# Three small networks' first layer: four products and a bias product become three products with the biases as rows

## The reference, cut to what matters

```python
U = (mu @ W_dec + b_dec).reshape(B, IN_DIM + 1, 30); param = einsum('bik,kj->bij', U, V)
x = x + (x @ param[:, :-1] + param[:, -1])
```

```python
def _mlp_ln(s, W1, b1, W2, b2, g, b):
    h = silu(s @ W1 + b1) @ W2 + b2
    return _ln(h, g, b)
m = x + _mlp_ln(memory_state, mem_W1, mem_b1, ...)[:, None, :]    # 256 inputs
n = x + _mlp_ln(noise_state, noi_W1, noi_b1, ...)[:, None, :]     # 64 inputs
r = x + _mlp_ln(resource_state, res_W1, res_b1, ...)[:, None, :]  # 32 inputs
```

## Time and profile before

| what | value |
| --- | --- |
| median of 3 runs | 608.56 us (607.65 to 608.61) |
| profiled execution | 608.91 us |
| its span, first to last instruction | 607.1 us |
| PE busy | 576.7 us, 95% |
| DVE, POOL, ACT busy | 431.5, 389.4, 200.1 us |
| granted TensorE clock, mean | 0.997 of full speed |

### The profile page before, as it was taken

One profiled execution on the slowest core, in us unless ns is written; L12 is line 12 of the kernel. 1 busy time (PEld: TensorE's weight loads), 2 busy tenths in 40 slices (PEclk: granted clock), 3 DMA queues, 4 the chain that ended last, 5 costly groups with the idle time before them and its releaser, 6 DMA issues.

```text
span 607.1 us, 9086 instructions
## 1 busy us (share of the span) xinstructions
PE 576.7 (95%) x2892; PEld 445.5 (73%) x2892; DVE 431.5 (71%) x781; ACT 200.1 (33%) x345; POOL 389.4 (64%) x499
## 2 busy tenths in 40 slices
PE   0999989899999999999999999999999999999995
PEld 0465546477777787777888888888888888888784
DVE  4311387589998899889866777777777777777854
ACT  4333453333333333433323223332233322332222
POOL 1011467568888888878866767667776777776720
PEclk9999999999999999999999999999999999999998
DMA  8999995424544444555535434444433333443201
GB/s 333 406 405 372 376 354 205 131 82 140 162 152 142 141 140 154 148 155 156 152 95 140 137 112 138 140 139 139 133 98 127 129 122 122 139 139 95 100 18 52
DMA packets 47967, 100.50 MB, mean 166 GB/s; under 512 B 9646, under 2 KB 19118, under 8 KB 47804
## 3 DMA queue, kind: packets, MB, share of 16 engines
q1 hardware_dynamic: 35424, 57.96, 27.5%
q0 software_dynamic: 12160, 42.04, 22.2%
q10 hardware_dynamic: 348, 0.06, 0.1%
HBM read 91.53 MB, written 8.39 MB: 165 GB/s over the span
## 4 chain that ended last, share of the span: by engine, by line
POOL 25%; DVE 23%; issue 20%; PE 10%; DMA 3%; ACT 1%; POOLq 1%; DVEq 1%
POOL h L1081 6%; DVE bn L1250 6%; POOL h L1079 6%; POOL ctt L1046 5%; DVE ops L1245 4%; DMA pwt<-in_pw,idx 3%; PE bank L751 3%; POOL rs L1029 3%; PE bank L753 3%; PE bank L752 3%; DVE x L1281 2%; POOL xop L1070 2%; DVE ht L1310 2%; DVE mv L1254 1%; POOL ve L1021 1%
## 5 line engine op out<-in xcount | busy, mean ns | idle before, releaser
L751 PE MATMUL bank<-W,ops 128*128 128x512 f32 x432 | 177.5, 411 | 1.1 <-DVE W L1218 0.3
L753 PE MATMUL bank<-W,ops 128*128 128x512 f32 x432 | 169.5, 392 | 0.0
L752 PE MATMUL bank<-W,ops 128*128 128x512 f32 x432 | 169.4, 392 | 0.0
L598 ACT ACTIVATE ops<-bank 128x512 fp32r<-128x512 f32 x97 | 56.9, 588 | 150.6 <-PE bank L745 148.9
L751 PEld LDWEIGHTS bank<-W,ops 128*128 128x128 f32 x432 | 81.6, 189 | 28.8 <-issue 10.4
L753 PEld LDWEIGHTS bank<-W,ops 128*128 128x128 f32 x432 | 81.4, 188 | 18.4
L752 PEld LDWEIGHTS bank<-W,ops 128*128 128x128 f32 x432 | 81.8, 189 | 14.1 <-issue 0.2
L1245 DVE TENSOR_TENSOR ops<-bank,ops 128x512 fp32r<-128x512 f32 x97 | 66.6, 687 | 10.6 <-ACT ops L598 8.8
L1250 DVE BATCH_NORM_STATS2 bn<-h 128x6 f32<-128x512 f32 x32 | 22.2, 693 | 55.2 <-POOL h L1081 55.2
L1021 POOL TENSOR_SCALAR ve<-mv 128x1 f32<-128x1 f32 x94 | 31.3, 333 | 33.8 <-DVE mv L1254 31.2
L649 ACT ACTIVATE xhat<-x,nm,rs 128x512 f32<-128x512 f32 x32 | 26.1, 815 | 77.2 <-POOL nm L1034 77.2
(11 more groups left out here) (142 smaller groups left out, 1065.7 us busy)
## 6 DMA issues: line engine op xcount, KB each, us to landing
ring<-in_W_dec SPq DMA_DIRECT2D x16, 960.0 KB, 11.9
x<-in_x SPq DMA_DIRECT2D x32, 256.0 KB
out<-xb SPq DMA_DIRECT2D x31, 256.0 KB
stash<-in_xT SPq DMA_DIRECT2D x30, 256.0 KB, 10.7
ring<-in_int_W SPq DMA_DIRECT2D x4, 1024.0 KB, 14.1
xraw<-in_xT SPq DMA_DIRECT2D x14, 256.0 KB
mnr_row<-in_mnr SPq DMA_DIRECT2D x3, 768.0 KB, 7.7
ring<-in_mlp_W SPq DMA_DIRECT2D x1, 1024.0 KB, 4.7
```

What stands on the lines that cost most here:

```text
L598: nc.scalar.activation(dst.rearrange("p c t -> p (c t)"), bank[:, :], ACT.Copy).then_inc(done, 1)
L751: nc.tensor.matmul(bank[:, :], op[:, HI, c, :], w[:, HI, c, :], start=start and c == 0, stop=False)
L752: nc.tensor.matmul(bank[:, :], op[:, HI, c, :], w[:, LO, c, :], start=False, stop=False)
L753: last = nc.tensor.matmul(bank[:, :], op[:, LO, c, :], w[:, HI, c, :], start=False, stop=stop and c == KC - 1)
```

## The change

The four chunks become three. The third now holds the second network's 64 inputs, the third network's 32 inputs and, at rows 96 to 98, three rows that pick the bias of each network: in `cond` a one in the two columns of that network, in `mlp_W1` the bias itself. The product with `hid` and the transfer of `mlp_b1` go. `mlp_W1` is 768 KB instead of 1024 KB, and the constants `cst` are 32 columns (16 KB in all) narrower. The wait of PE for `mlp_in` moves from the first-layer product to the one that reads `vec`, and asks for two transfers instead of three.

```diff
-AT_IDENT = AT_COND + 4 * Q
+AT_IDENT = AT_COND + 3 * Q
...
-            return s.rearrange("p (c n) -> p c n", n=D)
+            return s[:, 0:3 * D if item == MLP1 else KC * D].rearrange("p (c n) -> p c n", n=D)
...
-            load(act, mlp_in, (hid, d["mlp_b1"]), (vec, d["mlp_b2"]),
+            load(act, mlp_in, (vec, d["mlp_b2"]),
...
             wait_ring(pe, MLP1)
-            pe.wait_ge(mlp_in, 16 * 3)
-            for c in range(4):
-                nc.tensor.matmul(pM[0:C, :], cond[:, c, 0:C], staged(MLP1)[:, c, :], start=(c == 0), stop=False)
-            nc.tensor.matmul(pM[0:C, :], ident[0:C, 0:C], hid, start=False, stop=True).then_inc(mlp_used, 1)
+            for c in range(3):
+                last = nc.tensor.matmul(pM[0:C, :], cond[:, c, 0:C], staged(MLP1)[:, c, :], start=(c == 0), stop=(c == 2))
+            last.then_inc(mlp_used, 1)
             prefill(NPRE - 2)
...
             pe.wait_ge(ub_ready, 1)
+            pe.wait_ge(mlp_in, 16 * 2)
             nc.tensor.matmul(pSUM[0:C, :], ident[0:C, 0:C], vec, start=True, stop=False)
...
-    cond = chunks(put(2 * MU, Q, (0, 0, a["cond_512"].T), (MU, B, a["cond_64"].T),
-                      (MU + P, 2 * B, a["fside_Bx32_0"].T)))
+    cond = chunks(put(MU + P, Q, (0, 0, a["cond_512"].T), (MU, B, a["cond_64"].T), (MU + NOI, 2 * B, a["fside_Bx32_0"].T),
+                      (MU + NOI + RES, 0, np.repeat(np.eye(3, dtype=np.float32), B, axis=1))))
...
-        "mlp_W1": chunks(put(2 * MU, D, (0, 0, L1["mem_W1"]), (MU, 0, L1["noi_W1"]), (MU + P, 0, L1["res_W1"]))),
-        "mlp_b1": np.repeat(np.stack([L1[f"{m}_b1"] for m in mlps]), B, axis=0),
+        "mlp_W1": chunks(put(MU + P, D, (0, 0, L1["mem_W1"]), (MU, 0, L1["noi_W1"]), (MU + NOI, 0, L1["res_W1"]),
+                              (MU + NOI + RES, 0, np.stack([L1[f"{m}_b1"] for m in mlps])))),
```

## The result

The changed kernel takes 610.49 us (median of 7 runs, 609.62 to 611.48), the kernel before beside it 608.41 us (7 runs, 607.47 to 610.56). The ratio is 1.0036, with a 95% interval of 1.0023 to 1.0049: slower by 0.36%, more than the 0.2% that can be told here. The forecast was 607.9 us and a range up to 608.9; the measured time lies outside it. The profiled execution took 611.12 us, its span 609.3 us.

A forecast was written before the change was run, and what follows sets the result against it. PE was taken as the bound, busy for 95% of the span. Gains of 0.43 (embed), 0.07 (decode stage) and 0.20 (`Uf`) sum to 0.70 us, off 608.56: 607.9 us, range 606.8 to 608.9.

The forecast's parts named there:

- the term for `Uf`: Set-up transfers: with `mlp_W1` 256 KB shorter on SP's queue, `Uf` lands 0.20 us sooner, bounds 0 and 0.83.
- no cost needs another clock: Whole kernel: granted clock at 2.4 GHz nearly throughout, so all costs were taken at that clock.
- PE's saving: First layer on PE: one chunk (0.88 us) and the bias product (0.95 us) go, 1.83 us; used rows do not matter.
- The wait it runs into: Tile 0's embed: PE waits 1.40 us for `Ust`, so only 0.43 us of the saving is gained.
- the two ends that I had set: `Uf` transfers: waiting for queue turns gives 0; being counted only after SP's older data gives 0.64 us sooner.
- The decode stage: Ahead of the first layer: 28.7 KB fewer constants and `mlp_b1` bring PE and `Uf` 0.07 us sooner.
- What carries it on: Behind the embed: a chain without slack moves `tt` and the block-S product at 95.49 by the same 0.7 us.
- reaches the end in full: Tiles, at PE's pace: whatever time PE gains before them shortens the whole kernel by as much.
- Rivals 1 to 3: `Uf` moves with SP's bytes, 607.4 to 607.2, 0.20; whole saving arrives, 606.7, 0.10; swallowed by 95.49, 608.2 to 608.6, 0.12.
- Rival 4: Set-up: `Uf` lands 2.5 us later, at 73.2, embed at 74.9; 2.1 us slower, 610.6; chance 0.07.

The follow-up runs named there:

- e4: The changed kernel once more, unaltered; ratio interval to the kernel before 1.0033 to 1.0063, profiled execution 608.89 us.
- e2: Changed kernel with three products kept but all loads put back as before (`mlp_W1` in four chunks, wider `cond`, `mlp_b1` loaded); 608.90 us.
- e8: Changed kernel with 11 MATMULs of unused result filling PE's wait ahead of tile 0's embed; 0.21% slower than the kernel before.
- e3: Changed kernel with the front half of the last prefill moved ahead of tile 0's embed; 0.09% above the kernel before.
- e5: Changed kernel with `mlp_W1` alone padded to 1024 KB again; faster than the changed kernel, ratio not in the text.
- e6: Changed kernel with an unused 256 KB load right behind the 768 KB `mlp_W1`; faster than the changed kernel, `Uf` in at 70.58 us.
- e13: Changed kernel with POOL issuing tile 0's gathers only once ACT's `Uf` transfers are in; `Uf` in at 71.86 us, ratio not in the text.
- e14: Changed kernel with tile 0's gathers held until `Uf` is in and the last prefill's front half ahead of the embed; 0.08% above the kernel before.
- e7: Changed kernel with `mlp_W1` padded to 1024 KB and the last prefill's front half ahead of the embed; +0.05% against the kernel before.
- e10: Changed kernel with tile 1's `xraw` load (256 KB) moved ahead of block T; `Uf` in at 71.89 us, ratio not in the text.
- e12: Kernel before with tile 0's `x` load (256 KB) moved behind block T; `Uf` in at 70.77 us, ratio not in the text.
- e9: Changed kernel with SP's block T and later megabyte loads held back until `Uf` has landed; 1.0081 against the kernel before, median 613.48 us.
- e15: Kernel before with POOL issuing tile 0's gathers only once ACT's `Uf` transfers are in; ratio 0.9993.
- e1: Changed kernel with two extra products of unused result ahead of its three, loads as changed; PE's embed wait 2.08 us, ratio not in the text.
- e11: Changed kernel with tile 1's `xraw` load ahead of block T and the last prefill's front half ahead of the embed; ratio not in the text.

## Why the prediction was wrong, step by step

Two steps failed: the term for `Uf`, with 0.20 us sooner where 1.44 later was measured, and the sentence that no cost needs another clock, where the wait that the forecast itself had built let the clock fall to 1.2 GHz for 6.8 us.

- **PE's saving:** right. 1.69 us by the start of the prefill, 1.83 forecast; the used rows do not matter. One wait was not in the list: the prefill needs DVE's `ops`, for which PE waits 0.42 us in e4, 0.17 in e2 and 0.24 in e8. Where no wait shows (e3, e5, e6), the three chunks take 2.67 us and not 2.79 as here.
- **The wait it runs into:** right in place and kind. `ust_ready` is late next. Silu is not, and `x_lo`, ready at 69.95 + 1.29 = 71.24 where PE stood from 71.16, only by 0.08 us, hidden behind `Ust`. 1.40 us were forecast, 2.76 measured, because `Ust` itself came later. The release took 0.15 us, from the end of DVE's last copy at 73.36 + 0.41 = 73.77 to 73.92, where 0.06 was taken.
- **"What moves the `Uf` transfers": failed.** I took 0.20 us sooner, with bounds of 0 and 0.83 sooner. It came 1.44 later. The bounds had no end on the late side, and the chance of 0.07 on the rival rested on "the load on the engines is less". e5 and e6 show the reverse: 256 KB less in or behind `mlp_W1`, later `Uf`. Neither of the two ends that I had set, 0 and 0.64 us sooner, has the measured sign. By what means the landing moves stays open.
- **The decode stage, 0.07 us:** too small to be told. The first layer starts at 65.06 in both. Over all profiles here it starts at 64.82 to 65.06 without those bytes (65.54 in e13) and at 64.97 to 65.09 with them. `mlp_W1` itself landed 4.2 us after its issue instead of 4.7, as 256 KB less should, and that helped nobody.
- **"No cost below needs another clock": failed,** and this may be the larger part. The new wait lets the clock fall, as the profile shows, and in the mean of the executions it is lower. Mean clock 0.9978 to 0.9950 is 0.0028 x 609 / 0.5 = 3.4 us at the lower level in the mean, which loses half of that in work, 1.7 us. The measured loss is 2.1. That is an estimate and rather too high, because a low clock costs nothing while PE stands: e14 has a mean clock of 0.9957, which would be 1.3 us by the same sum, and is only 0.08% (0.5 us) above before. e4's profile without the fall is level with before, and e8, with the clock held, gets back 0.15 to 0.27% of the 0.36 to 0.48%. It was in no term and in no rival, although the forecast itself had built a wait of 1.40 us.
- **What carries it on:** right up to block S. `tt` and the block-S product moved with the embed, at a slower clock by more than it (+3.26 and +3.28 against +1.10). That a shift there "reaches the end in full" does not hold for a single execution: 3.28 became 2.2, and e4's 0.94 (96.43 against 95.49) became nothing.
- **The rivals.** Rivals 1 to 3 fell. Rival 4 had the sign and nearly the time (610.6 against 610.49), but for half of the reason: its landing at 73.2 would have moved the embed by 2.1; it landed at 72.1 and moved it by 1.1. The rest was the clock. That the time agrees so well was luck.
- **And without both mishaps?** e7 has neither a late `Uf` nor a wait at the embed, and still its interval, -0.05 to +0.16%, has no room for more than 0.3 us of the 1.83. Its profiled execution was short (span 605.9), but its mean clock over all runs is 0.9961, lower than before's. Its other waits behind the embed (1.64 us for `xop` of tile 1, 0.50 for `noi_W`) are longer than before's (0.81 and none). e14 is alike: 0.70 us at the embed, 1.6 for `xop`, and a mean clock of 0.9957. That these waits let the clock fall in the unprofiled runs is likely and not shown.

The Trainium skill, "TensorE: Matmul & The Clock Gate", section "HAM oscillation — how this bites in real kernels", describes a kernel whose short bursts of matmuls are followed by DMA waits of 3 to 5 us, and how the clock drops in these waits so that the next burst starts at the low rate. The rows above agree on the kind: the MATMULs at 74.91 to 79.17 are 0.43 us apart instead of 0.23. They differ in size: waits of 1.73 to 2.76 us were enough here. And at nearly the same wait in the same kernel it happened in one execution and not in another.

## What stays open

What the DMA queues do with the `Uf` packets. Shown are: the bytes decide and not the row size (e5, e6); bytes merely moved to or from the place ahead of block T do not (e10, e12); the megabytes altogether cost it at least 3 to 4.5 us (e9). Whether the place of the 256 KB counts or their sum, no run tells, and whether the gathers have a part in it is not shown. No rule that I could state gives all of it. Open is as well what makes the clock fall in one execution and not in another. A version that is faster than before was not found: e15, at 0.9993 with 1 inside its interval, is no gain that can be told.

## What to carry to other kernels

Work taken from a full engine is worth nothing where the next wait is just behind it, and less than nothing where that wait lets TensorE's clock fall: the gap is paid twice, and work moved (or merely put) into it can be worth more than the work removed. Where a small transfer is awaited behind megabyte loads, its landing can shift by a microsecond or two with an edit of the queue beside it (here 70.5 to 73.1 us), and in the direction one does not expect, so bound it on both sides, or give it its own time before the big loads are issued and check who then waits for these. Where a time scatters, put it beside the mean granted clock of each run before you explain it with the order of instructions: in e4, e5, e6 and e13 the two have a correlation of -0.72 to -0.94, in e3, e7, e8 and e14 of +0.17 to -0.26.

## What the hardware showed that I had not expected

- PE's waits at the embed and the lower level, 1.2 GHz, in the profiled executions: the clock fell at waits of 2.76, 2.08, 1.86 and 1.73 us (changed, e1, e13, e2), during the wait or up to 0.6 us after its end; it did not at 2.71, 2.32 and 2.01 (e10, e4, e5), nor at 1.4 and under (e3, e6, e8, e11, e14). It was down for 3.4 us in e1, e2 and e13 and for 6.8 us in the changed kernel; with e9's wait of 5.42 us, for 10.2 us.
- At that level a 128x512 MATMUL comes every 0.43 us instead of 0.23.
- Eight transfers of 7.5 KB took 7.8 to 10.3 us from ACT's first issue to DVE's start beside megabyte loads, 5.0 at most without them (e9).
- 256 KB more on one queue made the transfers of another come sooner: DVE starts at 70.5 to 71.2 us in seven profiles with them, at 71.4 to 73.1 in nine without.
